# Latent attention and a routed expert layer in one launch: maxima rows issued from ScalarE, expert choice in steps, and four smaller moves

## What is computed

```
c_kv = x @ W_DKV; k = c_kv @ W_UK; v = c_kv @ W_UV; q = x @ W_UQ
probs = softmax(causal(q k^T / 4)); x = x + (probs v) @ W_O
logits = norm(x) @ Wr / temp; topw, topi = top_k(logits, 2); topw = softmax(topw)
h = xf @ W1[e] + b1[e]; a, g = split(h)
out += (a * silu(g) @ W2[e] + b2[e]) * weight_e          # residual: x + out
```

## Time and profile before

| | us |
|---|---|
| median of 3 runs | 1365.41 (1365.27 to 1377.59) |
| profiled execution | 1362.01, its span 1359.9 |
| first score product of step 0 | 60.06 |
| turn 15 (step 194) | 775.44 |
| last context copy (after the last product) | 824.43 |
| first up-projection of the expert phase | 929.88 |
| PE busy, DVE busy, ACT busy | 1146.6 (84%), 750.2 (55%), 495.9 (36%) |
| mean granted TensorE clock | 0.796 of 2.4 GHz |

### The profile page before, as it was taken

How to read it: one execution, slowest core, us unless ns; L and a number is a source line. 1 busy time by engine, 2 the same in 40 slices (tenths; PEclk the granted TensorE clock), 3 DMA queues, 4 the chain that set the end, 5 groups by cost and what they waited for, 6 DMA issues and landing times. The chain is left out here.

```text
span 1359.9 us, 19012 instructions
## 1 busy us (share of the span) xinstructions
PE 1146.6 (84%) x5236; PEld 590.6 (43%) x5237; DVE 750.2 (55%) x2206; ACT 495.9 (36%) x1068; POOL 374.2 (28%) x459
## 2 busy tenths in 40 slices
PE   4399999979998969989679992506999999999995
PEld 2234443424443424444234430503666666666663
DVE  3277788544876645867648300433555555555553
ACT  1105776444554445646445450001222222222121
POOL 3003312423312723314223023040222222222222
PEclk9656999685866686857867555657999999999998
DMA  2944443364314374403743026625222222222222
GB/s 87 240 109 129 139 102 88 121 153 121 97 24 110 140 177 117 97 24 95 158 120 109 3 102 159 208 93 182 47 46 45 43 46 46 46 46 43 44 44 35
DMA packets 94889, 130.38 MB, mean 96 GB/s; under 512 B 26208, under 2 KB 71136, under 8 KB 94816
## 3 DMA queue, kind: packets, MB, share of 16 engines
q1 hardware_dynamic: 70304, 101.63, 27.6%
q0 software_dynamic: 13296, 17.77, 7.9%
q10 hardware_dynamic: 11216, 10.11, 2.7%
HBM read 74.60 MB, written 54.22 MB: 95 GB/s over the span
## 5 line engine op out<-in xcount | busy, mean ns | idle before, releaser
L1149 ACT ACTIVATE m_prob<-b_prob_ps 128x512 f32<-128x512 f32 (+3 forms) x768 | 340.8, 495 | 306.4 <-PE b_prob_ps L1262 300.7
L1262 PE MATMUL b_prob_ps<-m_stacks 50*128 50x512 f32 (+3 forms) x768 | 305.8, 493 | 49.3 <-DMA m_stacks<-b_max_rows 44.3
L1243 PE MATMUL b_max_ps<-m_stacks 48*128 48x512 f32 (+3 forms) x768 | 300.7, 493 | 45.5 <-DVE b_neg_max L827 22.9
L827 DVE CUSTOM_DVE_ANT_0 b_max_ps<-b_max_ps,b_mask_max 128x256 f32<-128x256 f32 (+3 forms) x512 | 247.6, 502 | 141.9 <-PE b_max_ps L1243 139.4
L1243 PEld LDWEIGHTS b_max_ps<-m_stacks 48*128 48x128 f32 x768 | 151.8, 234 | 264.3 <-DVE b_neg_max L827 126.4
L830 DVE TENSOR_REDUCE b_neg_max<-b_max_ps 128x1 f32<-128x512 f32 x256 | 176.3, 689 | 86.4 <-PE b_max_ps L1243 84.3
L1283 PE MATMUL b_acc_ps<-m_prob,b_v_aug 128*32 128x512 f32 (+3 forms) x1536 | 209.7, 628 | 1.3 <-POOL m_prob L686 1.3
L1577 POOL DMA_INDIRECT out_dram<-e_y,e_token x71 | 110.7, 1559 | 323.8 <-DVE e_y L1629 312.4
L686 POOL TENSOR_SCALAR_AFFINE_SELECT m_prob<-m_prob 128x512 f32<-128x512 f32 x128 | 80.5, 637 | 400.1 <-ACT m_prob L1149 399.6
L1262 PEld LDWEIGHTS b_prob_ps<-m_stacks 50*128 50x128 f32 x768 | 150.5, 236 | 89.5 <-DMA m_stacks<-b_max_rows 45.1
L1696 PE MATMUL e_g_ps<-m_w,e_rowsT 128*128 x284 | 135.6, 601 | 0.5 <-DVE e_rowsT L1597 0.5
(11 more groups left out here) (208 smaller groups left out, 1008.4 us busy)
## 6 DMA issues: line engine op xcount, KB each, us to landing
e_rows<-slot_rows ACTq DMA_DIRECT2D x73, 129.0 KB, 2.1
m_stacks<-q_parts SPq DMA_DIRECT2D x32, 256.0 KB, 5.5
m_stacks<-k_parts SPq DMA_DIRECT2D x32, 256.0 KB, 7.5
ctx_cols<-b_ctx_out SPq DMA_DIRECT2D x16, 512.0 KB
m_w<-in_L_ffn_W SPq DMA_DIRECT2D x8, 1024.0 KB, 7.9
k_parts<-a_part SPq DMA_DIRECT2D x14, 512.0 KB, 2.7
q_parts<-a_part SPq DMA_DIRECT2D x12, 512.0 KB, 3.2
m_stacks<-q_parts SPq DMA_DIRECT2D x32, 128.0 KB, 4.9
```

Of the source, the lines that this page charges most:

```text
L827: nc.vector.tensor_tensor_reduce(scores, scores, mask_max[:, HALF - width:HALF], -1.0, -MASKED, ALU.add, ALU.min, to).then_inc(max_done, 1)
L1149: nc.scalar.activation(prob[:, n % NP, 0:width], prob_ps[n % NS][:, 0:width], ACT.Exp, scale=SCALE).then_inc(prob_ok, 1)
L1243: nc.tensor.matmul(out_ps[:, 0:width], q_st[g % RING][at:at + STACK, j, i * P:(i + 1) * P], k_st[g % RING][at:at + STACK, j, half * HALF:h ...
L1262: nc.tensor.matmul(prob_ps[n % NS][:, 0:width], k_st[g % RING][at:at + MAXROWS, pair, j * P:(j + 1) * P], q_st[g % RING][at:at + MAXROWS, ...
```

## The change

The table of steps is changed, and with it who does what and when:

- `load_max_rows` moves from SP to ACT, right behind the copy that it sends.
- The choice of experts is cut into nine parts, one a step from slot 50, and the slots into six; the counting products move from slot 52 to 67, the scatter from 55 to 75 (for batch 2, which has no later maxima, both follow sooner). ACT copies the counts out of PSUM.
- `aux(s)` on PE comes after all four pairs of scores of a step.
- The first projections in the steps move from slots 7 and 19 to 17 and 29; in steps 0 to 15 and four times before them PE does a product that nobody reads (`keep_busy`).
- POOL's constants come before the start's work, and Wo, Wr and the temperature are issued by ACT with the first weights.
- `load_heads` waits for the denominators first and for the context later, one step sooner; the residual's load goes ahead of the spread; the spread is issued one step sooner; `load_stack(4)` comes at step 43 for 36.
- For the last batch the reciprocals are spread by 16 small matmuls with a 0/1 matrix that POOL makes at step 179.
- In the expert phase the biases of experts 1 to 7 wait for the first row tile.

```diff
-CHUNK_AT = [7, 19]
+CHUNK_AT = [7, 20]
+FIRST_CHUNK_AT = [17, 29]
...
-HEADS_AT, ADD_AT, NORMAL_AT = 27, 32, 44
-ROUTER_AT, COUNT_AT, SCATTER_AT = 48, 52, 55
+LOAD_AT, INVERT_AT, SPREAD_AT, HEADS_AT, ADD_AT, NORMAL_AT = 20, 23, 24, 28, 32, 44
+ROUTER_AT, CHOOSE_AT, COUNT_AT, SCATTER_AT = 48, 50, 67, 75
...
             def load_heads(b):
                 for p in range(2):
-                    sp.wait_ge(ctx_st[p], 32 * RING // 2 * (b + 1))
+                    sp.wait_ge(den_st[p], 16 * RING // 2 * (b + 1))
...
-            sp.dma_start(wo[:], w_o.rearrange("(c p) n -> p c n", p=P)).then_inc(small_in, 16)
...
-                if turned_at(s - 1) is not None:
-                    load_max_rows(turned_at(s - 1))
...
+                for g in range(1, NQUAD):
+                    if s == g * UNITS - (5 if g == RING else UNITS):
+                        load_stack(g)
...
-                if at_route(s, HEADS_AT - 2):
-                    spread_den(at_route(s, HEADS_AT - 2)[0])
-                    load_x2(at_route(s, HEADS_AT - 2)[0])
+                if at_route(s, SPREAD_AT):
+                    spread_den(at_route(s, SPREAD_AT)[0])
+                if at_route(s, LOAD_AT + 2):
+                    load_x2(at_route(s, LOAD_AT + 2)[0])
...
-            load_x2(LATE)
+                if s == LATE * PERIOD + PERIOD + 2:
+                    load_x2(LATE)
             load_heads(LATE)
-            spread_den(LATE)
...
+            def load_max_rows(g):
+
+                w = g % RING
+                act.wait_ge(rows_ok, g + 1)
+                for n in range(PARTS):
+                    for s in range(2):
+                        to = s * ROW_TILE + STACK + n
+                        of = n * HT + s * HT // 2
+                        act.dma_start(q_st[w][to:to + 1, :, :].bitcast(F32).rearrange("o j (t n) -> o (j t) n", n=P),
+                                      max_rows[g % 2][of:of + HT // 2, :]).then_inc(rows_in[w], 16)
...
                 if turned_at(s) is not None:
                     rows_copy(turned_at(s))
+                    load_max_rows(turned_at(s))
...
+            def keep_busy():
+
+                nc.tensor.matmul(aux_ps[:], ident[:], wo[:].rearrange("p c n -> p (c n)"), start=True, stop=True)
...
+                if s < LEAD:
+                    keep_busy()
...
+            def late_spread(k):
+
+                half, c = divmod(k, DC)
+                if k == 0:
+                    pe.wait_ge(inv_den_ok, BATCH)
+                    pe.wait_ge(late_const_ok, 1)
+                for t in range(TPC):
+                    last = nc.tensor.matmul(late_spread_ps[k][:, t * P:(t + 1) * P],
+                                            spread_to[:, c, half * TPC + t, :], inv_den[:], start=True, stop=True)
...
+            for n in range(START_BUSY):
+                keep_busy()
             pe.wait_ge(const_ok, ROUTE_CONSTS)
-            pe.wait_ge(small_in, 48)
...
-                    if q == 1:
-                        aux(s)
+                aux(s)
                 if 0 <= s - LEAD - LAG < TOTAL:
                     products(s - LEAD - LAG)
...
+                if e == 0:
+
+                    sp.wait_ge(rows_ok[0], 16)
```

More of the change, by code:

```diff
@@ L144, in at_route, with at_count @@
     return (batch, k) if 0 <= batch < LATE and k < count else None
+def at_count(step, first, count=1):
+    batch, k = divmod(step - first - PERIOD, PERIOD)
+    if 0 <= batch < LATE - 1 and k < count:
+        return batch, k
+    k = step - first + COUNT_AT - CHOOSE_AT - CHOOSE_STEPS - PERIOD * LATE
+    return (LATE - 1, k) if 0 <= k < count else None
 def aux_groups():
@@ L505, in load_heads @@
                     sp.wait_ge(aux_ps_ok, aux_at["router", b - 1] + 1)
+                for p in range(2):
+                    sp.wait_ge(ctx_st[p], 16 * RING // 2 * (b + 1))
                 context = dram["ctx"].rearrange("g (q s) n -> s (g q) n", s=2)[0]
@@ L732, in _ @@
                                     pattern=[[-1, P]], channel_multiplier=1).then_inc(ident_ok, 1)
+            constants()
             pool.wait_ge(w_order_in, 32)
@@ L1077, in _ @@
             late_turned(3)
-            choose_first(LATE)
-            choose_second(LATE)
-            weigh(LATE)
-            find_slots(LATE)
+            for part in range(CHOOSE_STEPS):
+                choose(LATE, part)
+            for part in range(FIND_STEPS):
+                find_slots(LATE, part)
             tables()
@@ L1119, in second_copy @@
             def second_copy(b, k):
-                act.wait_ge(xn2_ok, BT * (b + 1))
-                if b:
-                    act.wait_ge(second_in_slot, 16 * BT * b)
-                half = slice(k * PAIRS, (k + 1) * PAIRS)
-                nc.scalar.activation(second_row[:, half, 0:D], first_row[:, half, 0:D], ACT.Copy).then_inc(copy_ok, 1)
+                if k == 0:
+                    act.wait_ge(xn2_ok, BT * (b + 1))
+                    if b:
+                        act.wait_ge(second_in_slot, 16 * BT * b)
+                pair = slice(2 * k, 2 * k + 2)
+                nc.scalar.activation(second_row[:, pair, 0:D], first_row[:, pair, 0:D], ACT.Copy).then_inc(copy_ok, 1)
             def acc_copy(g, half):
@@ L1215, in _ @@
             late_turned(2)
-            for k in range(2):
+            for k in range(PAIRS):
                 second_copy(LATE, k)
             power_of(LATE)
+            count_copied(LATE)
         @block.tensor
```

220 lines of the change are left out of this document (127 added, 93 removed).

## The result

The changed kernel took **1429.5 us** (median of four, 1416.07 to 1437.93) against 1368.3 for the kernel before on the same chip: 1.040 of its time, interval 1.030 to 1.050 (here and below a median is of all executions of a kernel and a ratio of the undisturbed ones, so the two can differ a little). The forecast was 1275, range 1222 to 1330, chance of slower 0.04. It was wrong by 154 us and in its sign. The profiled execution has a span of 1414.3 us and took 1416.07; before they were 1359.9 and 1362.01.

A forecast was written before the change was run, and what follows sets the result against it. DVE sets the pace at full clock, PE at half clock, which costs the fused phase more than any wait. Terms 13 + 6 - 5 + 56 - 2 + 17 + 4 = 89 us off 1362.01 give 1273, as median 1275; range 1222 to 1330.

The forecast's parts named there:

- The step that failed: Steps 62 to 182: four DMA issues on ACT at each turn delay exponentials and PE runs dry; -12 us.
- Steps 62 to 182: Steps with rows of maxima, clock, choice in steps, ACT's issues and side work; sum +56 us.
- the side work's place: Steps 62 to 182: side work in one stretch gains at half clock, loses 0.3 us at full; -5 us.
- Start: Before step 0: it waits for the first stack and comes at about 47 instead of 60.06; 13 us.
- First 14 steps: At the full clock, with extra products fitting beside DVE, they take 37 us instead of 42.5; 6 us.
- Rows of maxima: Steps 62 to 182: ACT's issue removes SP's delays and queueing; of 44.3 us of waits 9 stay; +35 us.
- the first rival: Rows wait as long in flight as before, only late issue is saved; gain 53, time 1309 to 1312; chance 0.20.
- Clock recovery: Steps 62 to 182: half-clock stretches behind the waits for rows go, other drops stay; +30 us, bounds 0 and 74.
- Choice in steps: Steps 62 to 182: DVE's bursts of 1.5 to 5 us no longer hold three banks; +8 us, bounds 0 and 12.
- Tail: After the last copy: the first output projection begins near 838 instead of 855.5; +17 us, bounds 12 and 21.
- Expert phase: First row tile lands in about 2 us instead of 7.8 among the biases; +4 us, bounds 2 and 5.
- the last one: Rival: new stalls in the steps make the clock fall more often; slower, time 1451; chance 0.05.

The follow-up runs named there:

- 1: Changed kernel with the loads of the rows of maxima issued by SyncE again, one step behind the copy: 1353.0 us, ratio 0.990 to the kernel before.
- 9: Changed kernel with ScalarE's four issues for the rows of maxima spread, one behind each exponential: 1350.9 us, ratio 0.990 to the kernel before.
- 2: Kernel before with only the loads of the rows of maxima moved to ScalarE, four issues together: 1380.8 us, ratio 1.014 to the kernel before.
- 10: Kernel before with only the loads of the rows of maxima moved to ScalarE, one behind each exponential: 1340.5 us, ratio 0.979.
- 3: Changed kernel with the side work back behind the second pair of products of scores: 1353.7 us, ratio 0.984 to the kernel before.
- 12: Kernel 13 with the side work behind all four pairs, as in the change: 1318.9 us, ratio 0.959 to the kernel before.
- 11: Changed kernel with ScalarE's copy of the side work's result moved behind its fourth exponential: 1398.6 us, ratio 1.022 to the kernel before.
- 15: Changed kernel with only the extra products taken out: 1389.2 us, ratio 1.008 to the kernel before.
- 14: Kernel 13 with the choice of experts back in bursts: 1288.0 us, ratio 0.936 to the kernel before.
- 13: Changed kernel, side work behind second pair, no extra products, issues spread, no SyncE wait ahead of expert biases: 1279.6 us, ratio 0.933 to the kernel before.

## Why the prediction was wrong, step by step

The step that failed is in "Steps 62 to 182": "ACT can't start an exponential in that time, and PE has three banks of them, so it runs dry after about a microsecond. At each of ten turns I take 1.2 us: **-12**, bounds 0 and -24." The stall was foreseen, and its size nearly right (1.2 to 2.4 us of idle at the eleven turns reached at full clock, 1.6 as a rule). Its price was taken as the idle time alone, while the clock was a separate term of **+30** with the other sign, which came from the waits that went. In the trace after, at each of these eleven turns the clock falls behind the stall, for less than ten us at turn 4 and for 20 and more at turns 1, 2, 8, 12 and 13, and there are more turns than there were waits. By the ratios with and without it, the piece costs 69 to 70 us in the changed kernel (1, 9) and 48 in the kernel before (2, 10), not 12, and both lie outside the bounds.

The second failed term is the side work's place, **-5** with bounds -20 and +10: 78 us beside the issues in one piece (3), 36 without them (12). Its price at the full clock, 0.3 us a step, was near the 0.4 measured; the sum failed where it set this against a gain at the half clock, which no run shows, and where it left ScalarE out. That ScalarE's copy stays between the third and the fourth exponential, while what it copies now comes behind the fourth product, stands in the two kernels' code and was not weighed (11: 1.9%).

In the profiled executions the forecast was 143 us too low (1416 for 1273). Between turn 0 and turn 15 lie 124 of them, a loss of 73 where a gain of 51 was forecast; the first 14 steps have 18, and what is behind turn 15 came within 2 us. The other terms, in the prediction's order:

- Start, **13**: step 0 at 46.25 for 60.06, so 13.8. Right.
- First 14 steps, **+6**, bounds +6 and -5: they took 55.0 us for 42.5, so **-12.5**, outside the bounds. The row of 47 to 101 above has TensorE busy 50.75 of 54 us and the clock at 0.50. Up to step 0 it had stood at 1.00; it fell as the step began, behind 2.6 us in which TensorE waited for the last load of the stack:

```profile
44.00:46.00 2.00, 0.00 (x0) 1.00 1.01 272
46.00:48.00 2.00, 1.37 (x4) 0.51 1.05 408
```

  The group of the extra products from 38 to 110 (count, busy us, mean ns, idle before):

```profile
L1426 PE MATMUL x_aux_ps<-c_wo,b_ident 128*128 128x512 f32 x40 | 36.8, 1033 | 0.7 <-issue 0.7
```

  That is 20 calls of two records, 1.84 us each. The Trainium skill ("TensorE: Matmul & The Clock Gate", Part 1), by whose rule the term was +6, says that sustained matmul activity releases the throttled clock; this stretch, 94% busy at 0.50, does not bear that out. Without the extra products the same steps took 30.5 us, at 0.50 too (15). The prediction had their price at the half clock nearly right, "about 2 us a step", but took the full clock as likelier, at which they would have cost nothing.
- Rows of maxima, **+35**: the waits went whole, 44.3 us. But that they landed sooner is mostly not ScalarE's doing, and in this the first rival was right. At turn 5 the loads had taken 8.3 us. Here they are in the changed kernel (331.2 to 341.2), and below it in the kernel before with ScalarE as issuer (10, 294.6 to 304.6); in number 2 it was 9.1:

```profile
m_stacks<-b_max_rows ACTq DMA_DIRECT2D x4, 8.0 KB, 4.4
```
```profile
m_stacks<-b_max_rows ACTq DMA_DIRECT2D x4, 8.0 KB, 9.3
```

  With SyncE as issuer in the changed kernel (1) they took 5.9. So most of the difference goes with the rest of the change, perhaps with what else is in flight there; that was not tested. The Trainium skill ("DMA: Bandwidth & Descriptors", section "Issuing engines are not separate DMA queues") says that another issuer only saves issue time, and the 8.3 and 9.3 us of the kernel before agree. The rival's 20.8 us of saved waits was near for the part alone: of 44.3 us 18.1 stayed in number 10. POOL's masks and the spread, put at 3 us a batch, cost nothing.
- Clock recovery, **+30**, bounds 0 and 74: none of it came: 0.71 for 0.93 in the first four turns, 0.69 for 0.70 in the next eleven. Even with the stalls gone, rows on ScalarE gave the kernel before 29 us for the 65 of both terms (10): from turn 4 to turn 15 the clock was 0.72 for 0.70 in its profiled execution, the slowest of its five, so it falls at other places too. This is the third term that was too large.
- Choice in steps, **+8**: 8 by medians, 5 by ratios, not told apart from nothing (14).
- Tail, **+17**: from the last copy to the first output projection, by the timeline of the changed kernel:

```profile
897.87 0.60 ACT L1170 ACTIVATE b_ctx_out<-b_acc_ps 128x512 f32<-128x512 f32 x1 [2.47 <-PE b_acc_ps L1342]
...
903.67 0.95 DVE L874 RECIPROCAL c_inv_den<-c_den_in 128x128 f32<-128x128 f32 x1 [19.61 <-DMA c_den_in<-ctx_dens]
...
904.68 5.28 PE L1491 MATMUL b_max_ps<-c_inv_den,c_spread 128*128 128x128 f32 x24 [6.87 <-DVE c_inv_den L874]
...
909.07 1.88 DVE L927 TENSOR_TENSOR c_heads<-c_heads,b_max_ps 128x512 f32<-128x512 f32 x3 [4.45 <-DMA c_heads<-ctx_cols]
...
910.69 1.68 PE L1499 MATMUL b_prob_ps<-c_wo,c_heads 128*128 128x256 f32 x7
```

  12.8 us where there were 31.1, so 18. Right. The context's landing at 909 is last now, no longer the spread.
- Expert phase, **+4**: wrong in sign. The row tile landed soon (TensorE's first transposition at 976.4), but SyncE, having waited for it, stepped its semaphores late, as TensorE's timeline there shows:

```profile
976.38 0.66 PE L1765 MATMUL e_rowsT_ps<-e_ident,e_rows 128*128 128x128 f32 x2 [36.63 <-DMA e_rows<-slot_rows]
...
984.51 3.76 PE L1778 MATMUL e_g_ps<-m_w,e_rowsT 128*128 x4 [6.21 <-SPq L1644]
```

  The first up-projection came 8.1 us behind the first transposition; before it was 3.1 behind it (926.8 and 929.9), when the row tile had taken 7.8 us to land. Taking the wait out gave 3.7 us in the traces (13).

Of the rivals, the last one (chance 0.05) named both stalls and the clock at once and gave 1451 us for 1429.5. It had the place; that it nearly had the size is in part luck. It took all 113 steps at full clock for lost, while the clock was clearly lower only in the first four turns (0.71 for 0.93), and it left out what the extra products and VectorE's waits cost. It deserved more than 0.05, since the clock was known to fall behind waits in this very trace and the change added a stall at every turn.

What stays open: why the two parts together cost more than one by one, beyond the count above, and how much (33 us in the traces, 40 by the ratios); what shortened the rows' flight; and the 20 us of number 15.

## What to carry to other kernels

Where the profile shows stretches at half clock behind stalls, price each new stall by the stretch that may follow it and not by its own length: here 1.2 to 2.4 us of idle at a turn was worth 48 us in one kernel and 70 in the other. Before a DMA moves to an engine that computes, look for gaps of one issue (0.5 to 0.6 us) between its instructions and put one issue in each; four together stop all that waits for the engine. Don't expect the loads to land sooner for it. When work on one engine is put elsewhere in a step, move the instruction that takes its result on the next engine too, and see what the pace-setting engine does meanwhile.

## What the runs showed of the hardware

- A stall of one length can leave the clock alone or bring it down. Behind turn 1 the changed kernel's TensorE was busy 2.98 of 5 us, and the clock fell within the 1.61 us of idle. With the side work back (3) the stall there was even longer, 1.88 us for 1.61, with 3.12 of 5 us busy, and it held:

```profile
138.50:143.50 5.00, 5.00 (x33) 1.00 0.28 107
143.50:148.50 5.00, 3.12 (x19) 1.00 0.31 115
148.50:153.50 5.00, 4.29 (x34) 1.00 0.27 105
```

  There the projection stood ahead of the stall; in the changed kernel it stood behind it, and the window has 11 matmul records for 19. Over all turns of number 3 the clock held at 6 of 13.
- Work alone didn't lift it: 54 us with TensorE 94% busy at 0.50, behind a wait of 2.6 us that began at 1.00, in a kernel whose expert phase then has digits of 9 throughout.
- Four DMA issues in a row held ScalarE 2.51 us at the turn shown; spread they took 0.51 to 0.55 us each.
